# Expert-weight transposes issued inside the projection loop, and expert units ahead of attention units

## The reference

```python
def reference(x, qw, kw, vw, ow, Wg, We, be):      # x: (16, 2048, 1024) float16
    xn = _layernorm(x, axis=-1)
    # attention, 16 heads of 64, causal, scores / sqrt(1024), Q and K rotated
    s = softmax_causal(rope(xn @ qw) @ rope(xn @ kw).T / 32) @ (xn @ vw) @ ow
    # experts: We is (8, O, D) = (8, 1024, 1024) float32, Wg is (8, 1024)
    vals, sel = jax.lax.top_k(xn @ Wg.T, 2)
    w = jax.nn.softmax(vals, axis=1)
    y = jnp.einsum('td,eod->teo', xn, We) + be[None]
    f = jnp.einsum('tk,tko->to', w, jnp.take_along_axis(y, sel[:, :, None], axis=1))
    return x + s * silu(f)
```

## Time and profile before

| | us |
|---|---|
| median of the 2 runs shown | 3345.54 |
| lowest and highest of them | 3267.55, 3423.53 |
| the profiled execution | 3276.75 |
| its span on the slowest core (core 7) | 3275.2 |
| spans of the eight cores | 3239.0 to 3275.2 |

### The profile page before, as it was taken

The page is one execution under the profiler, slowest core; times in us unless marked ns, Lnnn a source line. Parts: engine busy times, 40 slices in busy tenths (PEclk is TensorE's granted clock), DMA queues, the critical chain, the costliest instruction groups (busy, mean ns, idle before and its releaser), DMA issues.

```text
span 3275.2 us, 31216 instructions; the slowest of 8 cores (3239.0 to 3275.2 us)
## 1 busy us (share of the span) xinstructions
PE 2180.9 (67%) x9976; PEld 800.5 (24%) x9976; DVE 999.3 (31%) x1529; ACT 1037.2 (32%) x1406; POOL 557.6 (17%) x727
## 2 busy tenths in 40 slices
PE   2777889001277588678858886277588588858886
PEld 1333335000022122223212222022123222212222
DVE  2566665003033233312221222033233313221222
ACT  3333442001111233243335444111233244334443
POOL 0455566000011111101010101011111101010010
PEclk9888998555599799879978998699799889969998
DMA  4777534883723312312230212522322302221111
GB/s 120 137 153 167 131 104 106 174 168 92 185 77 102 91 67 88 101 40 78 78 90 26 77 52 78 142 78 102 90 78 77 113 29 78 78 77 46 58 52 39
DMA packets 255822, 304.68 MB, mean 93 GB/s; under 512 B 179360, under 2 KB 187552, under 8 KB 255152
## 3 DMA queue, kind: packets, MB, share of 16 engines
q0 software_dynamic: 31552, 126.39, 13.7%
q10 hardware_dynamic: 66576, 102.78, 10.1%
q1 hardware_dynamic: 157536, 73.53, 9.5%
HBM read 218.50 MB, written 84.15 MB: 92 GB/s over the span
## 4 chain that ended last, share of the span: by engine, by line
PE 48%; DVE 13%; DMA 11%; ACT 9%; issue 8%; SPq 7%; ACTq 2%; DVEq 1%; POOL 1%; POOLq 0%
PE PB L716 28%; DVE AR L736 8%; SPq L238 6%; ACT AR L870 6%; DMA xq<-x_c 5%; PE PA L861 5%; DMA AR<-we 5%; PE PV L791 4%; PE PA L420 3%; PE PC L420 3%; PE PB L420 3%; ACTq L239 2%; DVE AR L813 1%; PE PC L687 1%; PE PV L360 1%
## 5 line engine op out<-in xcount | busy, mean ns | idle before, releaser
L716 PE MATMUL PB<-AR 128*128 128x512 f16 x4096 | 991.1, 385 | 201.8 <-DVE AR L736 201.6
L870 ACT ACTIVATE AR<-PA 128x1024 f16<-128x1024 f32 (+3 forms) x640 | 573.8, 897 | 1097.1 <-PE PA L861 1058.2
L736 DVE SCALAR_TENSOR_TENSOR AR<-PB,wm,AR 128x512 f32<-128x512 f32 x512 | 384.4, 751 | 1257.2 <-PE PB L716 1086.9
L716 PEld LDWEIGHTS PB<-AR 128*128 128x128 f16 x4096 | 377.6, 98 | 768.0 <-issue 390.7
L861 PE MATMUL PA<-AR 64*128 64x512 f16 x1280 | 269.8, 415 | 405.4 <-DMA AR<-q_sp 241.3
L880 POOL TENSOR_TENSOR AR<-AR,tri 128x256 f16<-128x256 f16 x256 | 170.8, 667 | 1739.9 <-ACT AR L870 1701.9
L791 PE MATMUL PV<-AR 128*128 128x512 f16 (+6 forms) x1280 | 368.4, 380 | 28.9 <-POOL AR L880 28.7
L861 PEld LDWEIGHTS PA<-AR 64*128 64x128 f16 x1280 | 67.9, 94 | 690.4 <-issue 690.4
L420 PE MATMUL PC<-AR 128*128 128x512 f16 x512 | 198.4, 387 | 0.0
L813 DVE COPY AR<-PV 64x1024 f32<-64x1024 f32 x64 | 77.8, 1216 | 337.1 <-PE PV L791 331.3
L929 PE MATMUL PA<-AR 128*128 128x512 f16 x512 | 136.6, 428 | 47.6 <-DVE AR L943 33.6
(11 more groups left out here) (95 smaller groups left out, 1565.3 us busy)
## 6 DMA issues: line engine op xcount, KB each, us to landing
AR<-weTsp POOLq DMA_DIRECT2D x128, 512.0 KB, 5.9
AR<-weTsp ACTq DMA_DIRECT2D x128, 512.0 KB, 5.7
we<-we POOLq DMA_DIRECT2D x8, 2048.0 KB, 17.8
weTsp<-AR ACTq DMA_DIRECT2D x32, 512.0 KB, 4.2
out_c<-AR SPq DMA_DIRECT2D x64, 256.0 KB, 2.9
v_sp<-AR POOLq DMA_DIRECT2D x32, 264.0 KB, 2.6
AR<-v_sp POOLq DMA_DIRECT2D x2, 4224.0 KB, 29.4
AR<-x_c SPq DMA_DIRECT2D x32, 256.0 KB, 5.3
```

Source lines behind the costliest of these rows:

```text
L716: sl=sl: e2.matmul(PB[:, 512 * be_:512 * be_ + 512], xnq[sl][:, c * 512 + t * 128: c * 512 + (t + 1) * 128], weT[be_][:, c * D + half * 51 ...
L736: e=e: e2.scalar_tensor_tensor(acc32[t][:, half * 512:(half + 1) * 512], PB[:, 512 * be_:512 * be_ + 512], wm32[:, gt * 8 + e:gt * 8 + e + 1],
L870: W("scalar", lambda e, sbk=sbk, ev=ev: e.activation(ev(expb3[sbk]), ev(PA), AF.Exp, scale=1.0 / 32.0), waits=[("swc", wcT), ("eT", C["eT" ...
```

## The change

Two edits. First, the 32 units leave their place behind the loop and become closures in a list; from pass 12 on, each pass of the loop of stage 1 issues the next two at its end. Their instructions, waits and buffers stay as they were. What is left after the loop is issued there; 16 passes take all 32, so nothing is. Second, in stage 2 the batch of `p2_units` that followed an attention unit is now issued before it.

```diff
--- before.py
+++ after.py
@@ -511,6 +511,35 @@
             dma("gpsimd", k_sp[s, t * 128:(t + 1) * 128, :],
                 kr_st[p][:, :], sk_, waits=[("eP", ropek)])
 
+        def _wtsp_fill(ee, c2, wbt):
+            sl2 = wbt % 2
+            wts = [("swe", 16 * (ee + 1)), ("swb", 32 * wbt)]
+            if wbt >= 2:
+                wts.append(("swc", 16 * (wbt - 1)))
+            for j in range(2):
+                c = c2 * 2 + j
+                dma("sync", bnc[sl2][:, j * 1024:(j + 1) * 1024],
+                    we16[ee, :, c * 128:(c + 1) * 128], "swb",
+                    transpose=True, waits=wts)
+                wts = []
+            dma("scalar", weTsp_h[ee, :, c2 * 2048:(c2 + 1) * 2048],
+                bnc[sl2][:, :], "swc",
+                waits=[("swb", 32 * (wbt + 1)), ("swc", 16 * wbt)])
+        wtsp_units = []
+        _wbt = 0
+        for ee in range(NE):
+            for c2 in range(4):
+                wtsp_units.append(
+                    lambda ee=ee, c2=c2, w=_wbt: _wtsp_fill(ee, c2, w))
+                _wbt += 1
+        _wti = [0]
+
+        def drain_wtsp(n):
+            while _wti[0] < len(wtsp_units) and n > 0:
+                wtsp_units[_wti[0]]()
+                _wti[0] += 1
+                n -= 1
+
         ln_s0(0)
         ln_s0(1)
         for it in range(NT + 8):
@@ -547,24 +576,10 @@
                 p1b(it - 8)
             if 6 <= it < NT + 6:
                 p1a(it - 6)
-
-        wbt = 0
-        for ee in range(NE):
-            for c2 in range(4):
-                sl2 = wbt % 2
-                wts = [("swe", 16 * (ee + 1)), ("swb", 32 * wbt)]
-                if wbt >= 2:
-                    wts.append(("swc", 16 * (wbt - 1)))
-                for j in range(2):
-                    c = c2 * 2 + j
-                    dma("sync", bnc[sl2][:, j * 1024:(j + 1) * 1024],
-                        we16[ee, :, c * 128:(c + 1) * 128], "swb",
-                        transpose=True, waits=wts)
-                    wts = []
-                wbt += 1
-                dma("scalar", weTsp_h[ee, :, c2 * 2048:(c2 + 1) * 2048],
-                    bnc[sl2][:, :], "swc",
-                    waits=[("swb", 32 * wbt), ("swc", 16 * (wbt - 1))])
+            if it >= 12:
+                drain_wtsp(2)
+
+        drain_wtsp(len(wtsp_units))
         wcT = C["swc"]
 
         for t in range(NT):
@@ -1001,11 +1016,14 @@
                 pu = p2_units(k)
                 j = 0
                 for i, u in enumerate(au):
-                    u()
                     share = ((i + 1) * len(pu)) // len(au)
                     while j < share:
                         pu[j]()
                         j += 1
+                    u()
+                while j < len(pu):
+                    pu[j]()
+                    j += 1
                 tok["qT_free"] = C["eT"]
                 combine(s, qg, k)
             tok["kT_free"] = C["eT"]
```

## The result

The changed kernel takes 3288.69 us at the median, the kernel before 3278.51 in the same comparison. The ratio is 1.0031, with a 95% interval from 1.0018 to 1.0044: some 10 us slower. The profiled execution took 3279.69 us, with a span of 3278.2 on its slowest core (core 4). Executions in which one half of the chip ran at a lower clock are left out of all comparisons; two of the experiments' profiles fell into one, and there the text uses the other half's cores alone.

A forecast was written before the change was run, and what follows sets the result against it. No engine is full in the hole behind stage 1's loop; a serial chain of transposes bounds it. 3276.75 - 174.5 (saving) + 88 (loop) + 75 (casts) + 12 (stage 2) = 3277 us, range 3185 to 3345.

The forecast's parts named there:

- the saving: Hole behind the stage 1 loop: without the 32 units there, the gate's Exp starts at 585.1 instead of 759.65, saving 174.5 us.
- The new loop: Stage 1, passes 12 to 27: ScalarE waits for the transposes, 21.4 us a quiet pass instead of 13.7; cost 88 us.
- The casts: Stage 1, passes 14 to 22: five casts hold up transposes in flight, net 15 us each, 75 us in all.
- Stage 2: Batches ahead of their attention units: 16 more table loads, 20.5 us of ScalarE, 12 us taken as cost; batch order itself free.
- The sum: Whole kernel: saving against loop, casts and stage 2 gives 3277 us; chance of within 2% was 0.57.
- The lighter loop: Stage 1: 20 us a pass (+65), 6 us a cast (+30), stage 2 +8; 3205 us, chance 0.25.
- The hidden transposes: Stage 1: transposes land before ScalarE's wait, only stage 2's 12 us stand against the saving; 3114 us, chance 0.10.
- The heavier loop: Stage 1: both legs at their upper rows, 10.2 and 15.9 us, 26.4 a pass (+168); 3357 us, chance 0.15.
- rival 1: Stage 1: the lighter loop, where a cast shares the DMA engines with the transposes; 3205 us, chance 0.25.

The follow-up runs named there:

- the last experiment: Kernel before, units still behind the loop, with the weTsp stores issued from SP instead of ScalarE's queue: ratio 0.9922 (0.9895 to 0.9949).

## Why the prediction was right and wrong

The forecast was no change, 3277 us, and the kernel became 10 us slower. The step that failed is the saving, which was put too high; the first edit's own net was forecast at -11.5 us and measured at -2 (-9 to +4), while the second edit's +12 was measured at +13 (8 to 18).

- **The saving** was the mis-sized term. It was worked out from the slowest core, 174.5 us, and on that core it was right: 201.7 us before, 26.7 after. But in that execution the slowest core was also the one with the longest hole; the mean over the cores is 166.7, and with the other two profiles of the old stage 1 it is 170.6 and 167.8. With 166.7 in its place the forecast's sum is +8.3 us, near the 10 measured.
- **The new loop** was right, in its mechanism and on the means of the cores. The prediction had 7.0 us from ScalarE's release to the first transpose, 14.0 for the two pairs and 0.35 for the store, 21.4 a pass. In passes 24 to 27 of the eight cores the first leg is 6.2 us on the mean and the second 14.7; the mean pass is 21.4. Single passes scatter (5.5 to 7.7, and 12.6 to 17.1): in the quiet pass above the two pairs take 528.98 - 512.64 = 16.3 us, and from the release at 529.31 to the next first transpose, 0.5 us behind the store of 534.32, it is 5.5. VectorE's L347 and L469, at 1.74 and 1.37 us before, take 0.49 and 0.42 in such a pass, since GpSimd works while ScalarE waits. The lower end of 6.1 us had left out L476, which takes 1.12 us in the pass of the earlier trace rows and 0.42 here.
- **The casts** were near in size, but they took another course. The forecast for the sixteen passes was 342 + 75 = 417 us, and 408.0 were measured. Taken from twelve passes at 21.4, passes 12 to 24 show 322.5 - 256.8 = 66 us for the casts where 75 stood. The prediction let a cast hold up the pair that was in flight, for a pass of 38 us and a next one of some 20. In the trace the cast issued at 264.40 on core 4 finds a pair in flight, which lands at 271.06, long before the cast (290.11). It is what the next pass issues that is held: the transpose issued at 277.33 lands at 295.98. Of two such passes the first takes 23.5 us and the second 32.2; the sum is 55.7 us, where 57.9 were forecast. So it is partly luck that the size came out.
- **Stage 2**: 12 us were predicted, 8.7 stand in the changed kernel's profile (8.9 between the profiles of the single edits) and 13 in the ratio of the second edit alone. The 16 loads are there to the number. Costing the batch order at nothing was not shown: with the Silus last it is worth 14 us, and whether the second edit's 13 us is a larger loss by the loads less a small gain by the order is open.
- **The sum** was +0.5 us and the measurement says about +10, in the class "within 2%" that had the largest chance, but in a direction that was not forecast: two terms of over 160 us of opposite sign were subtracted, and 8 us of one of them are enough to decide the sign. The two profiled executions themselves differ by only 4.1 us on the mean (the loop came 2 us and stage 2 3 us under their terms), and such means move by 4 to 11 us from one execution to another. So the size of the missed term is known to some us only; that the first edit brings less than forecast stands on its ratio.
- **The rivals.** The lighter loop did not come (21.4, not 20, and the casts cost 66). The hidden transposes did not, since ScalarE's wait is real. The heavier loop did not either: its legs were 10.2 and 15.9 us, and 6.2 and 14.7 were measured. The rule of the Trainium skill ("DMA: Bandwidth & Descriptors", Queues, rings and completion order) on queues taking turns packet by packet would have given rival 1. The trace has casts that land after 24.1 us in place of 17.6 and a pass of 32.2 us, so both sides give way, and neither an even share nor a full stop fits.

## What to carry to other kernels

A transfer that waits for another transfer belongs on a queue whose engine computes nothing, and in a dose that fits into the slack of that queue. Here that brought the quiet passes back to 13.6 us; beside the casts the passes stayed uneven. Moving it from behind a loop into the loop only helps if nobody in the loop has to stand in line behind its wait. When two large terms cancel, work each from the mean of all cores and not from the slowest, and look at cheap orderings elsewhere: keeping the Silus together, four lines, was worth 0.4% in the old order of stage 2 and 1.6% in the new one.

## What the runs showed of the hardware

- A table load and a Silu between two exps cost their full time: with the 36 loads and 32 Silus out of the attention of stage 2 its stretches are 77.9 us shorter, against 80.1 us of ScalarE's own time, though ScalarE is busy for only a third of the span. In the end stage 2 is 43 us shorter, 1.2 us for each load of 1.283. The Trainium skill ("ScalarE: Activation LUTs", What ACT_TABLE_LOAD costs) gives 1.283 us, which the rows confirm, and about 1.38 us of drain on top, 2.66 in all. The rows above show the next activation 0.01 us after the load's end and the load at most 0.08 us behind the activation before it, and the effect of 1.2 us a load includes no second 1.38.
- Casts and transposes that share the DMA engines cost more together than apart, by 36 us over twelve passes. A cast issued less than 1.35 us behind a transpose in flight can take 30 to 62 us to land, with everything that is issued meanwhile, where 21 is the median: 27 of 62 such casts did, in the kernels with one unit a pass, and one of the other 194. Cutting the casts in halves made the kernel slower (0.9661 against 0.9547).
- In one execution of the kernel with one unit a pass, four cores were granted a TensorE clock of 0.74 to 0.76 over 60 us of stage 1 while the other four had 1.00, with quiet passes of 15.0 us against 13.6 on the mean. Cores 0 to 3 of the last experiment show the like, 0.80 to 0.86 from 370 to 430 us. Its cause is open.
